# Gate product with its weights four times over, layer norm by tokens along the free axis, corners of the band in one transpose

## The reference

```python
xn = layernorm(x)                       # over the 128 features, no weights
h  = relu(xn @ nm_w1 + nm_b1);  m = h @ nm_w2 + nm_b2
q, k, v = m @ q_w + q_b, m @ k_w + k_b, m @ v_w + v_b
att = softmax(q . k over keys j with |i - j| <= 32, scale 128**-0.5) @ v
gates  = xn @ gate_w.T                  # 16 experts
scores = sigmoid(gates)
# the 8 experts with the highest scores + expert_bias; their scores over their sum, times 2.826
ffn = sum_e combine_e * (silu(xn @ w_gate_e) * (xn @ w_up_e)) @ w_down_e
ffn += (silu(xn @ shared_gate) * (xn @ shared_up)) @ shared_down
out = x + att + ffn
```

## Time and profile before

| | us |
|---|---|
| median of 3 runs (lowest, highest) | 715.92 (715.48, 717.18) |
| the profiled execution: its time, its span | 715.54, 713.4 |
| busy in the span: PE | 702.2 (98%) |
| PEld | 577.4 (81%) |
| DVE | 573.1 (80%) |
| ACT | 440.6 (62%) |
| POOL | 405.3 (57%) |

### The profile page before, as it was taken

The page is one execution under the profiler, slowest core; times in us unless marked ns, Lnnn a source line. Parts: engine busy times, 40 slices in busy tenths (PEclk is TensorE's granted clock), DMA queues, the critical chain, the costliest instruction groups (busy, mean ns, idle before and its releaser), DMA issues.

```text
span 713.4 us, 10683 instructions
## 1 busy us (share of the span) xinstructions
PE 702.2 (98%) x3412; PEld 577.4 (81%) x3412; DVE 573.1 (80%) x1598; ACT 440.6 (62%) x878; POOL 405.3 (57%) x363
## 2 busy tenths in 40 slices
PE   8889999999999999999999999999999999999997
PEld 6668888888888888888888888888888888888886
DVE  6888787887878888788887878878788887878775
ACT  5766665656665576655657566566665766656573
POOL 4785665555556555666555555554656546555463
PEclk9999999999999999999999999999999999999999
DMA  7606144071621506134061421516125061430600
GB/s 260 208 0 221 62 129 154 5 247 33 206 77 46 228 10 239 45 109 175 2 236 45 178 104 35 219 30 237 46 79 203 2 236 45 150 117 8 247 0 16
DMA packets 36519, 83.67 MB, mean 117 GB/s; under 512 B 7152, under 2 KB 15600, under 8 KB 36464
## 3 DMA queue, kind: packets, MB, share of 16 engines
q1 hardware_dynamic: 36464, 83.00, 33.7%
HBM read 78.27 MB, written 4.72 MB: 116 GB/s over the span
## 4 chain that ended last, share of the span: by engine, by line
PE 94%; DVE 3%; ACT 2%; issue 0%; DMA 0%; POOL 0%; DVEq 0%
PE ps_y L406 26%; PE ps_u L396 26%; PE ps_g L386 26%; PE bank L321 3%; PE bank L363 3%; PE bank L344 3%; PE bank L326 2%; PE bank L353 2%; PE bank L333 2%; PE ps_y L372 1%; DVE ps_u L997 1%; DVE h_lo L1003 1%; ACT h_hi L631 0%; DMA xin<-x 0%; DVE xn L755 0%
## 5 line engine op out<-in xcount | busy, mean ns | idle before, releaser
L1085 POOL TENSOR_TENSOR silu_c<-silu,comb_b 128x512 f32<-128x512 f32 x256 | 330.7, 1294 | 291.1 <-ACT silu L623 289.5
L631 ACT ACTIVATE h_hi<-ps_u 128x512 fp32r<-128x512 f32 x272 | 162.5, 597 | 258.4 <-DVE ps_u L997 256.4
L1003 DVE TENSOR_TENSOR h_lo<-ps_u,h_hi 128x512 fp32r<-128x512 f32 x272 | 185.8, 683 | 59.7 <-ACT h_hi L631 59.5
L997 DVE TENSOR_TENSOR ps_u<-silu_c,ps_u 128x512 f32<-128x512 f32 x256 | 176.9, 691 | 44.5 <-PE ps_u L396 38.7
L623 ACT ACTIVATE silu<-ps_g 128x512 f32<-128x512 f32 x272 | 161.5, 594 | 1.7 <-PE ps_g L386 1.5
L396 PE MATMUL ps_u<-xn_hi,exp_w_hi 128*128 128x512 f32 x272 | 110.5, 406 | 4.7 <-DVE h_lo L1003 4.7
L406 PE MATMUL ps_y<-h_hi,exp_w_hi 128*128 128x512 f32 x272 | 112.6, 414 | 0.4 <-DVE h_lo L1003 0.4
L386 PE MATMUL ps_g<-xn_hi,exp_w_hi 128*128 128x512 f32 x272 | 108.1, 397 | 0.0
L386 PE MATMUL ps_g<-xn_lo,exp_w_hi 128*128 128x512 f32 x272 | 107.8, 396 | 0.0
L386 PE MATMUL ps_g<-xn_hi,exp_w_lo 128*128 128x512 f32 x272 | 107.6, 396 | 0.0
L406 PE MATMUL ps_y<-h_hi,exp_w_lo 128*128 128x512 f32 x272 | 107.5, 395 | 0.0
(11 more groups left out here) (146 smaller groups left out, 992.1 us busy)
## 6 DMA issues: line engine op xcount, KB each, us to landing
comb_b<-c_dram SPq DMA_DIRECT2D x63, 1024.0 KB, 8.9
xin<-x SPq DMA_DIRECT2D x16, 256.0 KB, 3.4
xres<-x_t SPq DMA_DIRECT2D x16, 256.0 KB, 2.9
out_t<-xres SPq DMA_DIRECT2D x16, 256.0 KB, 2.0
exp_raw<-wexp SPq DMA_DIRECT2D x2, 960.0 KB, 10.8
c_dram<-comb_t SPq DMA_DIRECT2D x64, 8.0 KB, 1.8
exp_raw<-wexp SPq DMA_DIRECT2D x1, 768.0 KB, 7.6
exp_raw<-wexp SPq DMA_DIRECT2D x1, 384.0 KB, 5.4
```

What stands on the lines that cost most here:

```text
L631: A(h_t[hbuf(par, s)][0][:], ps_u[(par + s) % 2][:], ACT.Copy).then_inc(s_h_hi, 1)
L997: V.tensor_tensor(ps_u[i][:], src[:], ps_u[i][:], ALU.mult).then_inc(s_h, 1)
L1003: V.tensor_tensor(t[1][:], ps_u[(par + s) % 2][:], t[0][:].bitcast(F32), ALU.subtract)\
L1085: G.tensor_tensor(silu_c[i][:].rearrange("p (l x) -> p l x", l=2), silu[i][:].rearrange("p (l x) -> p l x", l=2), comb_b[:, :, s1 - 1, :], ...
```

## The change

1. **Gate product.** `gate_w` holds its 32 columns (16 hi, 16 lo) four times over, 128 columns, and is now the side that is loaded into the array; xn (hi, lo) is the moving side with all 512 tokens. Two matmuls instead of eight. The result has experts on the partitions, the same 32 rows four times. DVE's `gate_sum` turns it over: from each block of 32 partitions `j` it transposes the 128 columns of tokens 128j to 128j+127 in 32x32 blocks into `gate_h`, and then adds the halves as before. Partition 32j+k, place a now has token 128j+32a+k.
2. **Combine weights.** In that order `comb_t` has each token run of 64 as it is needed, so one transfer stores it. `comb_b` has eight runs of 64 tokens per expert (`RUNS`) instead of two of 256; `silu_c` and the spreads go by these.
3. **Layer norm, groups 3 and up** (`TURNED` = 3). x by tokens (now four successive tokens to a partition) is read for its moments alone. Mean and rstd of all 512 tokens are stored to DRAM and read back to all partitions (`mom_b`); x with features on partitions is loaded from `x_t` into `xn`; POOL subtracts the mean in two halves (`centre`, slots 14 and 15) and multiplies by rstd (`normalise`, slot 16) two groups ahead. PE's four transposes and DVE's `normalise` fall away; `xn_hi` and `xn_lo` read SBUF. `inverse_std` moves from POOL's slot 16 to slot 7. The moments move from DVE's slots 12 and 14 (group g+2) to 12 and 13 (group g+3), and group 3's own are taken in group 1, slots 4 and 5. `xn_lo` moves from slot 2 to 3 in all groups but the first.
4. **Corners.** `prob_n` has one row of 384 per sequence, the window of the first tile at 0, that of the second at 224 (`APART`). The two corner blocks of 32 keys share the middle block of 128 columns, so that three transposes do for four.

```diff
-        gate_w = sb("gate_w2", [P, 2 * E], F32R)
+        gate_w = sb("gate_w4", [P, 4, 2 * E], F32R)
-        prob_n = sb("prob_n", [P, TILES, SEQ])
+        prob_n = sb("prob_n", [P, NB, 3 * P])
-        comb_b = sb("comb_b", [P, 2, E, SEQ])
+        comb_b = sb("comb_b", [P, RUNS, E, T // RUNS])
...
@@ sync
+            def load_turned(g):
+                if g == TURNED:
+                    sp.wait_ge(S["xn_tp"], g)
+                else:
+                    sp.wait_ge(S["xn_lo"], g)
+                sp.dma_start(flat(xn), x_t[:, g * T:(g + 1) * T]).then_inc(s_xt, 16)
+
+            def spread_moments(g):
+                n = g - TURNED + 1
+                sp.wait_ge(S["rstd"], g + 1)
+                sp.wait_ge(S["mean"], n)
+                sp.dma_start(st_dram.rearrange("k (p a) -> p k a", p=P), mom[:]).then_inc(s_mom_st, 16)
+                sp.wait_ge(s_mom_st, 16 * n)
+                if n > 1:
+                    sp.wait_ge(S["xn"], g)
+                sp.dma_start(mom_b[:], st_dram.rearrange("(o k) t -> o k t", o=1).to_broadcast([P, 2, T]))\
+                    .then_inc(s_mom_b, 16)
...
-                for q in range(4):
-                    sp.dma_start(c_dram[par, :, :, q * 32:(q + 1) * 32],
-                                 comb_t[q * 32:(q + 1) * 32, :].rearrange("p (h t) -> p h t", h=2))\
-                        .then_inc(s_comb_st[par], 16)
+                sp.dma_start(c_dram[par], comb_t[:]).then_inc(s_comb_st[par], 16)
...
+                if s == 5 and TURNED <= g + 2 < GROUPS:
+                    load_turned(g + 2)
+                if s == 8:
...
+                    if TURNED <= g + 2 < GROUPS:
+                        spread_moments(g + 2)
@@ tensor
-                for a in range(TILES):
-                    for n in range(2):
-                        done = mm(bank[0][:, a * 2 * E:(a + 1) * 2 * E], xn_t[par][n][:, a * P:(a + 1) * P],
-                                  gate_w[:], start=n == 0, stop=n == 1)
+                for n in range(2):
+                    done = mm(bank[0][:], gate_w[:].rearrange("p q c -> p (q c)"), xn_t[par][n][:],
+                              start=n == 0, stop=n == 1)
...
-                for kb in range(2):
-                    for t in range(2):
-                        c = kb * (SEQ - (P - HALF)) + t * P
-                        done = nc.tensor.transpose(dst[:, c:c + P],
-                                                   prob_n[:, 2 * seq + t, kb * P:(kb + 1) * P], ident[:])
+                for n in range(3):
+                    done = nc.tensor.transpose(dst[:, n * P:(n + 1) * P], prob_n[:, seq, n * P:(n + 1) * P],
+                                               ident[:])
...
-                if s == when(g, 1, 5) and more:
+                if s == when(g, 1, 5) and g + 1 < TURNED:
                     pe.wait_ge(S["xn"], g + 2)
@@ vector
+                if g >= TURNED:
...
+                    V.tensor_copy(mom[:, 0, :], mv[:, :, 0]).then_inc(S["mean"], 1)
...
                 dve.wait_ge(S["gate_mm"], g + 1)
-                both = bank[0][:, 0:TILES * 2 * E].rearrange("p (a n e) -> p a n e", a=TILES, n=2)
-                V.tensor_reduce(gate_s[:], both.rearrange("p a n e -> p a e n"), AX.X, ALU.add)\
+                for j in range(4):
+                    rows = slice(j * 32, (j + 1) * 32)
+                    done = V.transpose(gate_h[rows, :, :].rearrange("p a c -> p (a c)"),
+                                       bank[0][rows, j * P:(j + 1) * P])
+                done.then_inc(S["gate_h"], 1)
+                dve.wait_ge(S["gate_h"], g + 1)
+                V.tensor_reduce(gate_s[:], gate_h[:].rearrange("p a (n e) -> p a e n", n=2), AX.X, ALU.add)\
                     .then_inc(S["gate_s"], 1)
...
-                if s == when(g, 2, 6) and more:
+                if s == when(g, 3, 6) and more:
                     xn_lo(g + 1, 1 - par)
@@ gpsimd
+            def centre(g, half):
...
+                c = slice(half * T // 2, (half + 1) * T // 2)
+                G.tensor_tensor(flat(xn)[:, c], flat(xn)[:, c], mom_b[:, 0, c], ALU.subtract)\
+                    .then_inc(S[f"centred{half}"], 1)
+            def normalise(g):
...
+                G.tensor_tensor(flat(xn), flat(xn), mom_b[:, 1, :], ALU.mult).then_inc(S["xn"], 1)
...
-                    G.tensor_tensor(silu_c[i][:].rearrange("p (l x) -> p l x", l=2),
-                                    silu[i][:].rearrange("p (l x) -> p l x", l=2),
+                    G.tensor_tensor(silu_c[i][:].rearrange("p (l x) -> p l x", l=RUNS),
+                                    silu[i][:].rearrange("p (l x) -> p l x", l=RUNS),
                                     comb_b[:, :, s1 - 1, :], ALU.mult).then_inc(s_silu_c, 1)
...
+                if TURNED <= g + 2 < GROUPS:
+                    if s == 7:
+                        inverse_std(g + 2)
+                    if s == 14:
+                        centre(g + 2, 0)
+                    if s == 15:
+                        centre(g + 2, 1)
```

More of the change, by code:

```diff
@@ L197, in layer @@
         s_stored = [sem(f"y_stored{i}") for i in range(2)]
-        names = """bn aggr var_eps rstd xn xn_tp xn_hi xn_lo gate_mm gate_s gate_e
+        names = """bn aggr var_eps rstd mean centred0 centred1 xn xn_tp xn_hi xn_lo gate_mm gate_h gate_s gate_e
             gate_1 score select top8 rest weight wsum winv comb comb_t
@@ L237, in flat, with windows @@
             return t[:].rearrange("p a d -> p (a d)")
-        def halves(b):
-            return b[:].rearrange("p (t c) -> p t c", t=2)[:, :, 0:WIN]
+        def windows(b):
+            return b[:, 0:2 * APART].rearrange("p (t c) -> p t c", t=2)[:, :, 0:WIN]
+        gate_raw = att_raw[:, GATE:GATE + E].rearrange("p (o e) -> p o e", o=1).to_broadcast([P, 4, E])
         @block.sync
@@ L245, in load_x @@
             def load_x(g, par):
-                sp.dma_start(xin[par][:], x[g * T:(g + 1) * T, :].rearrange("(a p) d -> p a d", p=P))\
-                    .then_inc(s_xin[par], 16)
+                rows = x[g * T:(g + 1) * T, :]
+                rows = rows.rearrange("(a p) d -> p a d" if g < TURNED else "(p a) d -> p a d", p=P)
+                sp.dma_start(xin[par][:], rows).then_inc(s_xin[par], 16)
+            def load_turned(g):
[14 more added lines that the diff above has]
+                    .then_inc(s_mom_b, 16)
             def load_res(g, par):
@@ L298, in slot @@
                         load_res(g + 1, 1 - par)
-                    if not last(g, 1):
+                    if first(g):
                         sp.wait_ge(S["xn"], g + 1)
                         load_x(g + 2, par)
+                    elif not last(g, 2):
+                        if g + 1 < TURNED:
+                            sp.wait_ge(S["xn"], g + 2)
+                        else:
+                            sp.wait_ge(S["bn"], g + 2)
+                        load_x(g + 3, 1 - par)
+                if s == 5 and TURNED <= g + 2 < GROUPS:
+                    load_turned(g + 2)
+                if s == 8:
+                    if first(g):
+                        sp.wait_ge(S["xn"], g + 2)
+                        load_x(g + 3, 1 - par)
+                    if TURNED <= g + 2 < GROUPS:
+                        spread_moments(g + 2)
                 if s == 13 and not last(g):
@@ L581, in xn_hi @@
             def xn_hi(g, par):
-                act.wait_ge(S["xn_tp"], g + 1)
-                A(xn_t[par][0][:], bank[1][:], ACT.Copy).then_inc(S["xn_hi"], 1)
+                if g < TURNED:
+                    act.wait_ge(S["xn_tp"], g + 1)
+                else:
+                    act.wait_ge(S["xn"], g + 1)
+                A(xn_t[par][0][:], bank[1][:] if g < TURNED else flat(xn), ACT.Copy).then_inc(S["xn_hi"], 1)
             def gate_exp(g):
@@ L617, in prob_hi @@
                 act.wait_ge(S[f"pt{seq}"], g + 1)
-                A(p_t[0][:, seq, :, 0:WIN], halves(score_bank[seq]), ACT.Copy).then_inc(S[f"p{seq}_hi"], 1)
+                A(p_t[0][:, seq, :, 0:WIN], windows(score_bank[seq]), ACT.Copy).then_inc(S[f"p{seq}_hi"], 1)
             def gate_silu(g, par, s):
@@ L653, in fresh_weights @@
                 act.wait_ge(s_fresh_mm, e + 1)
-                A(comb_b[:, :, e, :], src[:].rearrange("p (l x) -> p l x", l=2), ACT.Copy).then_inc(s_fresh, 1)
+                A(comb_b[:, :, e, :], src[:].rearrange("p (l x) -> p l x", l=RUNS), ACT.Copy).then_inc(s_fresh, 1)
             def fresh_att(s):
@@ L913, in normalise_probs @@
                 for t in range(2):
-                    c = t * (P - HALF)
-                    done = V.tensor_scalar(prob_n[:, 2 * seq + t, c:c + WIN], prob[:, 2 * seq + t, :],
+                    c = t * APART
+                    done = V.tensor_scalar(prob_n[:, seq, c:c + WIN], prob[:, 2 * seq + t, :],
                                            row_inv[:, 2 * seq + t:2 * seq + t + 1], None, ALU.mult)
@@ L928, in att @@
                     fresh_att(s)
-                if s == when(g, 0, 3) and more:
```

(17 more changed lines are left out.)

60 lines of the change are left out of this document (45 added, 15 removed).

## The result

The changed kernel takes 700.28 us (median of 4 runs, 699.49 to 700.38) against 715.80 of the kernel before on the same chip: ratio 0.9778, 95% interval 0.9764 to 0.9793. That is faster, as forecast, and 1.3 us under the 701.6 of the forecast. By the ratio it is 0.9778 x 715.8 = 699.9 us, 1.7 us under the forecast and just outside its range of 700.0 to 711.5. The parts that make up this sum were further off than the sum, in both directions.

The account below looks back on a forecast made before the run. The prediction took TensorE, busy 98% of the span, to bound the kernel. 715.54 - 15.6 (PE's savings) + 0.5 (prologue) + 0.8 (group 1) = 701.2 us, with 0.4 for the median 701.6; range 700.0 to 711.5.

Parts of the forecast that it names:

- TensorE bounds it and saved products count in full: Steady groups: PE has no idle time, so a microsecond off its stream is worth a microsecond if nothing else becomes late.
- Together 15.6 us: PE's savings: gate 6.3, transposes of xn 5.8, corners 3.5 us, if PE stays without idle time.
- without the losses at the ends it is 700.3: Forecast time without the prologue's 0.5 us and group 1's 0.8 us loss; lower end of the forecast's own 700.3 to 703.7.
- Prologue ... Minus 0.5 us: Start of the run: PE gains 0.4 us, but DVE's gate sum is 0.7 us later; net loss 0.5 us.
- Minus 0.8 us: Group 1, slots 4 and 5: group 3's moments and variance on DVE exceed the cover of ACT's Exps; loss 0.8 us.
- I take 0.22 us each: DVE's gate sum, slot 5: four 32x128 transposes out of PSUM at 0.22 us each, 0.95 us for the four.
- rival 1: Gate sum at its slow end, 0.31 us a transpose: PE stalls 0.2 us in 14 groups, 704.4 us; chance 0.12.
- the shift of 0.05 us: ACT's table load for the gate's Exp waits for the logits and so shifts by only some 0.05 us.
- Rival 2: POOL's rstd, moved to slot 7, blocks DVE's second prob_n of slot 8: 9.1 us in 13 groups, 710.7 us; chance 0.19.
- Rival 3: Eight runs cost POOL its fixed 146 ns each, silu_c 0.88 us longer: 24 us in 15 groups, 725.6 us; chance 0.06.
- Transfers: Combine-weight spreads in 1 KB instead of 4 KB runs: at most 2 us more per MB, 2.3 us in hand, so nothing.
- The forecast then added 0.4 us for the median over the profiled run: Final step: the median of the runs is 0.4 us above the profiled one, so 701.2 becomes 701.6.

Follow-up runs that it names:

- experiment 9: The kernel after with one untouched tile of 32 bytes a partition ahead of xn_hi: 702.20 us.
- experiment 5: The kernel before with one untouched tile of 32 bytes a partition ahead of the layer norm outputs: 713.04 us.
- experiment 8: The kernel after with group 0 alone taking gate product and gate sum as in the kernel before: 699.24 us.
- experiment 7: The kernel after, with POOL's fourth exp_w_lo of the prologue waiting for the combine weights of group 0: 699.42 us.
- experiment 2: The kernel before with the three-transpose corners alone: 712.44 us.
- experiment 12: The kernel after with POOL's fourth exp_w_lo waiting for group 0's combine weights, and group 3's moments and variance moved to slots 2 and 3 of group 1: 698.64 us.
- experiment 3: The kernel before with the gate part alone (product by experts, transposes on VectorE, combine weights in eight runs): 711.39 us.
- experiment 4: The kernel before with the layer norm part alone: 707.87 us.
- experiment 10: The kernel after with two more 32x128 VectorE transposes in the gate sum of groups 1 to 15: 708.05 us.
- experiment 11: The kernel after with one more POOL product of 128x256 in slot 7 of groups 1 to 13, between silu_c(8) and rstd: 704.52 us.
- experiment 6: The kernel before with both tiles that the layer norm part adds (32 and 4096 bytes a partition), never touched: 712.98 us.
- experiment 13: The kernel before with one untouched tile of 64 bytes a partition in place of the layer norm part's tiles: 715.34 us.

## Why the prediction was wrong, and where it was right

- **TensorE bounds it and saved products count in full**: right. Corners 0.22 us a group (forecast 0.22), gate 0.41 alone (0.42), layer norm 0.60 alone, of which the addresses make 0.18, so 0.42 (0.44).
- **The step that failed: "Together 15.6 us"**, a sum that takes the pitch of every product left, 0.233 us, as fixed. With the new tile addresses its mean fell, by 0.15 to 0.18 us a group (experiments 9 and 5), some 1.9 to 2.3 us in 13 groups. No row before could show that; but it was a term that I did not have, and "without the losses at the ends it is 700.3" was therefore no floor.
- **"Prologue ... Minus 0.5 us", with group 0**: the second step that failed, mis-sized. With the 0.64 us that the sum has for group 0 (0.42 for the gate product, 0.22 for the corners), group 1 should have started 0.14 us sooner; it started 1.52 later. The prologue's gate sum cost 1.24 us (experiment 8 against the kernel after: 66.75 and 67.99), 0.9 of it by the collision with POOL that I had not seen (experiment 7: 67.07). Slots 8 to 11, that I had at nothing, cost 0.74. The gate product gave its 0.43, the corners nothing in group 0 (experiment 2: +0.07). 1.24 + 0.74 - 0.43 = 1.55, as measured but for 0.03.
- **"Minus 0.8 us" in group 1**: right in size and reason (experiment 12: 0.81 us back; the layer norm part alone, 42.86, does not have the loss: it takes moments and gate sum together). That the group's 43.21 us meets 43.03 + 0.8 - 0.64 = 43.19 is in part luck: by the savings of experiments 2 to 4 in this group (42.81, 42.63 and 42.86 us for it), pitch included, experiment 12 should have had 42.2 us and had 42.40, and this other 0.2 us of loss, which is not explained, hides the gain of the pitch.
- **"I take 0.22 us each"**: wrong, 0.32 us; my upper bound was the true value. By rival 1 that meant a stall of 0.2 us a group and 704.4. There was none, since two errors met: I had let ACT's table load wait for the logits (the shift of 0.05 us), and it starts without them, so that they could have come 0.92 us later (290.87 and 291.79). No stall, but by luck, with 0.09 us to spare (experiment 10).
- **Rival 2** (rstd holds prob_n, 710.7): refuted, the pair takes 0.66 us beside rstd, though POOL's large products do hold DVE (experiments 7, 8, 11). **Rival 3** (eight runs cost POOL, 725.6): refuted, silu_c 1294 ns before and after. **Transfers**: the spread lands after 12.6 us, 3.7 more for its MB, where I allowed 2; it is the run length, since the gate part alone has 12.4 us and the layer norm part alone 8.8. No wait of POOL for it shows in the steady groups.

In sum: 701.2 on the profiled run, -2.3 (steady groups, nearly all of it the pitch), +1.7 (group 0), -0.3 outside the span (2.1 before, 1.8 after): 700.3, as measured. The forecast then added 0.4 us for the median over the profiled run, and there was no such difference after (700.28 and 700.29). Two errors of some 2 us had nearly cancelled.

## What to carry to other kernels

Where an engine is busy 98% of the time with equal instructions, its pitch is a term of its own: try a pad of 32 bytes in the tile list; one line was here worth 1.9 to 2.7 us, where the corners brought 3.4. Price the first pass apart from the steady one: an instruction that is covered in every later group lies bare there, and a shift of tenths decides whether it meets another engine's long product. When an expected stall does not come, measure the slack that is left before calling the model right.

## What the runs showed of the hardware

- A group of some 200 products, most of them float32r of 512 columns, took 42.86 instead of 43.03 us when the tiles from xn_hi on started on a multiple of 64 bytes instead of 32 over it (experiments 5, 6 and the kernel before), 43.01 when they started 32 over the next one (13). One kind of product has most of it, 233.3 to 225.1 ns from its start to the next.
- A 32x128 transpose on VectorE out of PSUM takes 0.30 to 0.32 us, and they do not overlap (four in 1.28). The pair of 32-column ones out of SBUF takes 0.31 for both the earlier trace rows.
- Beside a POOL product of 384 columns a VectorE instruction of 64 columns with its inputs in SBUF took 1.03 instead of 0.22 us; beside POOL's power on 128x4, 1.05 us long, a prob_n took its usual 0.29 us.
- The same MB in runs of 1 KB instead of 4 KB lands after 12.6 instead of 8.9 us (median of 63), 12.4 with the gate part alone.
